# Graph network on one Trainium2 core: edge counts shared with ScalarE, ranking by predicated copies in five parts, chunk tables beside the ranking

## The reference

```python
h = jnp.maximum(_layernorm(x, axis=-1), 0.0)
# layer 0: row = src, col = dst
edge_input = jnp.concatenate([h[row], h[col], edge_attr, edge_weight / 5.0], axis=-1)
m_ij = silu(silu(edge_input @ ew1 + eb1) @ ew2 + eb2)
agg = segment_sum(m_ij, row, num_segments=n)
x = x + h + silu(concatenate([h, agg]) @ nw1 + nb1) @ nw2 + nb2
# then two attention layers over (src, dst), softmax per dst; x = x + the result
```

## Time and profile before

| | us |
|---|---|
| median of 3 runs | 8896.73 (8894.26 to 8897.62) |
| span of the profiled execution, first to last instruction | 8886.9 |
| around the span (median less span) | 9.8 |

### The profile page before, as it was taken

One profiled execution on the slowest core, in us unless ns is written; L12 is line 12 of the kernel. 1 busy time (PEld: TensorE's weight loads), 2 busy tenths in 40 slices (PEclk: granted clock), 3 DMA queues, 4 the chain that ended last, 5 costly groups with the idle time before them and its releaser, 6 DMA issues.

```text
span 8886.9 us, 230055 instructions
## 1 busy us (share of the span) xinstructions
PE 6173.7 (69%) x49885; PEld 5210.5 (59%) x50563; DVE 6168.8 (69%) x25428; ACT 4847.6 (55%) x11854; POOL 6191.5 (70%) x7562
## 2 busy tenths in 40 slices
PE   2466666666599999984666666666646666666665
PEld 2365656556588888873555555545445555656564
DVE  7799833333267676757999999999856666666665
ACT  4133333333245555534777777777647777777775
POOL 0377777777777777735777777777647777777775
PEclk9988888888899999986888888888755555555555
DMA  4233222222232323312222222222421111111114
GB/s 141 52 63 63 62 63 62 63 62 62 61 90 85 86 85 86 85 35 56 55 55 55 55 55 55 56 55 56 47 25 29 29 29 29 29 29 29 29 29 28
DMA packets 990923, 493.64 MB, mean 56 GB/s; under 512 B 830674, under 2 KB 841604, under 8 KB 990276
## 3 DMA queue, kind: packets, MB, share of 16 engines
q0 software_dynamic: 168832, 302.29, 15.6%
q1 hardware_dynamic: 701892, 169.48, 10.2%
q10 hardware_dynamic: 119840, 18.68, 1.3%
HBM read 356.53 MB, written 151.48 MB: 57 GB/s over the span
## 4 chain that ended last, share of the span: by engine, by line
issue 26%; POOL 21%; PE 20%; DVE 15%; DMA 7%; ACT 7%; DVEq 3%; ACTq 1%; POOLq 0%; SPq 0%; another core or an unknown queue 0%
POOL z_s L639 13%; POOL arena L689 8%; DMA arena<-table,arena 6%; PE ps_all L961 5%; PE ps_all L971 5%; ACT arena L825 3%; PE ps_all L984 3%; PE ps_all L981 2%; DVE arena L1494 2%; PE ps_all L1069 1%; ACT arena L857 1%; DVE arena L1580 1%; PE ps_all L993 1%; DVEq L385 1%; DVE ps_all L1232 1%
## 5 line engine op out<-in xcount | busy, mean ns | idle before, releaser
L689 POOL DMA_INDIRECT arena<-table,arena x3616 | 3527.3, 975 | 1421.4 <-issue 963.9
L639 POOL DMA_INDIRECT z_s<-arena x1660 | 1591.9, 959 | 850.8 <-issue 479.6
L1093 PE MATMUL ps_all<-arena 128*128 128x132 f32 (+1 forms) x7232 | 1584.7, 388 | 1.8 <-DVE acc L1597 1.8
L1093 PEld LDWEIGHTS ps_all<-arena 128*128 128x128 f32 x7232 | 1405.9, 288 | 2.7 <-issue 2.6
L1069 PE MATMUL ps_all<-ident_b,arena 128*128 128x128 bf16 x3616 | 465.3, 270 | 1311.8 <-DMA arena<-table,arena 1191.7
L825 ACT ACTIVATE arena<-lanes_b,arena 128x128 bf16<-128x128 bf16 x3616 | 1144.9, 386 | 349.1 <-DVE arena L1467 342.2
L1069 PEld LDWEIGHTS ps_all<-ident_b,arena 128*128 128x128 bf16 x3616 | 282.3, 117 | 1478.6 <-issue 844.4
L1494 DVE TENSOR_REDUCE arena<-ps_all 128x2 f32<-128x1024 f32 x904 | 1098.5, 1215 | 39.0 <-PE ps_all L1110 37.6
L849 ACT ACTIVATE arena<-ps_all 28x512 bf16<-28x512 bf16 (+1 forms) x904 | 527.5, 584 | 956.8 <-PE ps_all L1069 955.8
L744 ACT ACTIVATE arena<-ps_all 18x512 f32<-18x512 f32 x415 | 243.3, 586 | 1211.9 <-PE ps_all L948 1180.1
L1110 PE MATMUL ps_all<-arena,pick 128*128 128x512 bf16 x1809 | 694.6, 489 | 54.6 <-DVE arena L1494 24.3
(11 more groups left out here) (259 smaller groups left out, 15032.7 us busy)
## 6 DMA issues: line engine op xcount, KB each, us to landing
arena<-z_s SPq DMA_DIRECT2D x452, 264.0 KB, 2.7
arena<-table,arena POOLq DMA_INDIRECT x3616
arena<-rec_d SPq DMA_DIRECT2D x1660, 10.0 KB
z_s<-arena POOLq DMA_INDIRECT x1660
rec_d<-in_rec ACTq DMA_DIRECT2D x1, 16160.0 KB, 59.0
arena<-ids_d SPq DMA_DIRECT2D x904, 4.0 KB
arena<-pos_d SPq DMA_DIRECT2D x830, 0.5 KB
arena<-pos_d ACTq DMA_DIRECT2D x830, 0.5 KB
```

The lines of the kernel that those rows point to most:

```text
L639: pool.indirect_dma_start(z_s, bass.IndirectOffsetOnAxis(ap=slot[:, g.slot(SLOTS), u:u + 1], axis=0), z_out[:, g.slot(SLOTS), u, :], None) ...
L689: pool.indirect_dma_start(g_rows[:, r, u * step + CODE_WORDS:(u + 1) * step], None, tables[n], bass.IndirectOffsetOnAxis(ap=ids[:, r, 0, u ...
L1093: mm = pe.matmul(ps[6][:, 0:out_w], a_hot_f[:, g.slot(4), u, :], g_msg[:, g.slot(4), u * out_w:(u + 1) * out_w], start=(u == 0), stop=(u = ...
```

## The change

- The counts: VectorE counts 42 of the 50 source tiles; ScalarE counts the last eight with nine Sign passes over `key`, then counts `bucket`. ScalarE's own-product copies are moved in between the Sign passes, one batch after every third.
- TensorE makes all own products first, then the prefix sums, one set per count: `prefix(1)` (sources), then `prefix(0)` (destinations).
- Ranking: five parts of 186, 186, 248, 496, 496 columns. A step is compare, scan into PSUM, carry, and `copy_predicated` of the scan's result into `place` where the compare hit; the carry and the copy wait for the scan only, and the compare's tile alternates between two, so that the next compare waits for nothing.
- 24 steps of part 0 run first; then VectorE takes up the destination counts and makes tile groups, gaps, base and the three comparisons with the tile ends; then come the other 25 steps. TensorE's table matmuls run beside these.
- In the edge loop part 1 gets two steps an item for three rounds, parts 2 to 4 one step an item for six rounds each.
- `x_t` is cleared by POOL after the last Sign pass; of `z_out` only the three last columns of each row are cleared.
- The index loads are cut in five pieces instead of four.

```diff
-PARTS = (310, 434, 434, 434)
-PART_ROUNDS = 6
-RANK_STEPS = 5
+PARTS = (186, 186, 248, 496, 496)
+RANKS_A_STEP = (0, 2, 1, 1, 1)
+FIRST_RANKS = 24
+SRC_BY_ACT = 8
+RANK_STEPS = 4
...
+            pool.wait_ge(S("signs_ready"), NB + SRC_BY_ACT + 2)
+            pool.memset(x_t, 0.0).then_inc(S("x_t_clear"), 1)
             pool.wait_ge(S("blanked"), 16 * NB)
...
-            act.wait_ge(S("bucket_ready"), 1)
-            for t in range(NB + 1):
-                act.activation(hit, bucket, ACT.Sign, bias=signs_at[:, t:t + 1], accum_out=signs[:, t:t + 1]).then_inc(S("signs_ready"), 1)
-                act.wait_ge(S("signs_ready"), t + 1)
...
+            act.wait_ge(S("key_ready"), 1)
+            for t in range(SRC_BY_ACT + 1):
+                at = NB - SRC_BY_ACT + t
+                act.activation(hit, key, ACT.Sign, bias=signs_at[:, at:at + 1], accum_out=src_signs[:, t:t + 1]).then_inc(S("signs_ready"), 1)
+                act.wait_ge(S("signs_ready"), t + 1)
...
+                if t % 3 == 2 and t // 3 < len(BATCHES):
+                    own_batch(t // 3)
...
-            with link.loop(NB, 1) as b:
+            by_dve = NB - SRC_BY_ACT
+            with link.loop(by_dve, 1) as b:
...
+            def rank(k, tile, ran, turn):
...
+                found = src_hit[turn][:, 0:PARTS[k]]
+                counted = (first_counted_ps if k == 0 else counted_ps)[:, 0:PARTS[k]]
+                nought = zero if k == 0 else zero_ps
+                dve.tensor_scalar(found, keys, no, None, ALU.is_equal).then_inc(small, 1)
+                dve.wait_ge(small, ran + 1)
+                dve.tensor_tensor_scan(counted, found, nought.broadcast_to([P, PARTS[k]]), come, ALU.add, ALU.add).then_inc(small, 1)
+                dve.wait_ge(small, ran + 2)
+                dve.tensor_scalar(come, counted[:, PARTS[k] - 1:PARTS[k]], 1.0, None, ALU.mult).then_inc(small, 1)
+                dve.copy_predicated(places, found.bitcast(I32), counted).then_inc(small, 1)
...
+            with dve.Fori(0, FIRST_RANKS // 2) as b:
+                for turn in range(2):
+                    rank(0, b * 2 + turn, b * (2 * RANK_STEPS) + turn * RANK_STEPS, turn)
...
-            link(dve.memset(x_t, 0.0))
-            dve.sem_inc(S("x_t_clear"), 1)
-            link(dve.memset(z_out, 0.0))
-            assert PART_ROUNDS * SLOTS == NT - 1
-            edge_pipeline(dve, SUPER, 0, bring, cuts=[(k * PART_ROUNDS, next_part) for k in range(len(PARTS))])
+            link(dve.memset(z_out[:, :, :, F_HID + 1:], 0.0))
+            edge_pipeline(dve, SUPER, 0, bring, cuts=[(RANK_ROUND[k], next_part) for k in range(len(PARTS))])
```

More of the change, by code:

```diff
@@ L137 @@
 PART_ENDS = [(at * P // GE - SLOTS) // SLOTS for at in PART_AT]
+RANK_ROUND = [sum((NT - 1) // (SLOTS * RANKS_A_STEP[k]) for k in range(1, n)) for n in range(1, len(PARTS) + 1)]
+assert all((NT - 1) % (SLOTS * n) == 0 for n in RANKS_A_STEP[1:])
 def edges_of(a, k):
@@ L714, in own_copies, with own_batch @@
                 act.activation(own_src[:, cols, :].rearrange("p t f -> p (t f)"), ps[4][:, 0:m], ACT.Copy).then_inc(S("own_copied"), 1)
[L717 to L724 removed]
+            def own_batch(b):
+                n = len(BATCHES[b]) * P
                 act.wait_ge(S("own_t"), b + 1)
@@ L868, in _, with prefix @@
             pe.matmul(ps[6][:, 0:1], ones, falls, start=True, stop=True).then_inc(S("falls_summed"), 1)
-            pe.wait_ge(S("counts_ready"), 2)
-            for k in range(2):
+            def prefix(k):
+                pe.wait_ge(S("counts_ready"), 2 - k)
                 pe.matmul(ps[7][:, 128 * k:128 * k + NB], lower, counts[k], start=True, stop=True)
                 pe.matmul(ps[7][:, 128 * k + 64:128 * k + 64 + NB], ones, counts[k], start=True, stop=True)
-                mm = pe.matmul(ps[7][0:NB, 256 + k:257 + k], counts[k], ones[:, 0:1], start=True, stop=True)
@@ L876, in _ @@
[L876 removed]
+                pe.matmul(ps[7][0:NB, 256 + k:257 + k], counts[k], ones[:, 0:1], start=True, stop=True).then_inc(S("prefix_ready"), 1)
             pe.wait_ge(S("weights_in"), 16 * (N_WEIGHTS + 1))
             pe.wait_ge(S("h_ready"), 1)
[L879 to L895 removed]
@@ new lines, in own_transposes, with own_products @@
+            def own_transposes(b):
+                if b > 1:
+                    pe.wait_ge(S("own_tt"), b - 1)
+                for u, t in enumerate(BATCHES[b]):
+                    mm = pe.transpose(ps[b % 2][0:F_IN, u * P:(u + 1) * P], hs[:, t, :], ident)
+                mm.then_inc(S("own_t"), 1)
+            def own_products(b):
+                pe.wait_ge(S("own_tt"), b + 1)
+                if b > 0:
+                    pe.wait_ge(S("own_copied"), 2 * b)
+                for u, t in enumerate(BATCHES[b]):
+                    pe.matmul(ps[2 + b % 2][:, u * F_HID:(u + 1) * F_HID], tile_t[0:F_IN, b % 2, 0, u * P:(u + 1) * P],
+                              w_dst, start=True, stop=True)
+                    mm = pe.matmul(ps[4][:, u * F_HID:(u + 1) * F_HID], tile_t[0:F_IN, b % 2, 0, u * P:(u + 1) * P],
+                                   w_src, start=True, stop=True)
+                mm.then_inc(S("own_done"), 1)
@@ L897, in _ @@
+            own_transposes(0)
+            for b in range(len(BATCHES)):
+                if b + 1 < len(BATCHES):
+                    own_transposes(b + 1)
+                own_products(b)
+            prefix(1)
+            prefix(0)
             pe.wait_ge(S("tile_groups_ready"), 1)
@@ L1250, in _ @@
             link(dve.tensor_scalar(reached[0:NB, :], group_no[0:NB, :], tile_end[:, 0:1], None, ALU.is_ge))
+            for k in range(2):
+                link(dve.tensor_scalar(reached_groups[k], numbers, tile_end[:, k + 1:k + 2], None, ALU.is_ge))
             dve.sem_inc(S("reached_ready"), 1)
+            with dve.Fori(0, (NT - FIRST_RANKS) // 2) as b:
+                for turn in range(2):
+                    rank(0, b * 2 + (FIRST_RANKS + turn), b * (2 * RANK_STEPS) + (FIRST_RANKS + turn) * RANK_STEPS, turn)
+            rank(0, NT - 1, (NT - 1) * RANK_STEPS, 0)
+            ranked(0)
             lone = ROW_CHUNKS // 4
@@ L1334, in bring @@
                 dve.tensor_tensor(slot[:, g.slot(SLOTS)], to_spare, slot_in[:, r], ALU.add).then_inc(small, 1)
-                if 0 < ranking[0] < len(PARTS) and g.i is not None:
-                    first = SLOTS + (ranking[0] - 1) * PART_ROUNDS * SLOTS
-                    rank(ranking[0], g.at - first, g.at * RANK_STEPS + (RANK_STEPS * (NT * ranking[0] - first)))
+                k = ranking[0]
+                if 0 < k < len(PARTS) and g.i is not None:
+                    first, each = SLOTS + RANK_ROUND[k - 1] * SLOTS, RANKS_A_STEP[k]
+                    for n in range(each):
+                        tile = g.at * each + (n - first * each)
+                        rank(k, tile, g.at * (each * RANK_STEPS) + RANK_STEPS * (NT * k + n - first * each),
+                             (n if each == 2 else g.off) % 2)
             ranking = [0]
```

107 lines of the change are left out of this document (40 added, 67 removed).

## The result

The changed kernel is **slower**, by half a per cent: 8939.24 us (median of 4 runs, 8937.75 to 8943.66) against 8897.17 (4 runs, 8894.26 to 8898.97), a ratio of 1.0052 with a 95% interval of 1.004 to 1.0064. The forecast was 8816 us, faster.

The account below looks back on a forecast made before the run. POOL's scatters bound the edge loop at a fixed 2097 us, behind VectorE's preamble chain. Ranking start -21.5, steps -53.1, middle +8.5, tables -14.9 give -81 us from 8896.7: forecast 8816 us, range 8800 to 8850.

Parts of the forecast that it names:

- the time of the change is the shift of SP's first load, unless the loop slows down: Whole kernel: edge loop is a fixed 2097 us train, so the gain is the shift of SP's first record load, to 254.5.
- the clock: Rival: TensorE's stage from 2600 to 3800 us gets clock 0.84 instead of 1.00, adding 255 us: 9071 us; chance 0.02.
- A batch gives TensorE three Sign passes to be ready in, so I take no further wait: Counts in the preamble: 5.3 us a batch suffices for TensorE's own products, so VectorE goes on at 150.0 us.
- counts done: Preamble: VectorE's 42 tile counts and two small operations end at 146.0 us.
- compare to compare: Ranking in the preamble: a step takes 1.43 us instead of 2.56, plus 0.1 per loop turn; -53.1 us in all.
- predicated copy: Ranking step: copy takes 0.36 us at 186 columns, less 0.09 overlap; taken from the addition's row.
- the middle: Between the two halves of part 0's ranking: destination counts, prefix sums, moved block and comparisons add 8.5 us.
- tables: From ranking's end to SP's first record load: 19.0 us instead of 33.9, -14.9 us.
- the last of the blank groups: SP's 50 blank groups, 82.7 us, end at 236.1, 0.6 us after part 0 is ranked; costs nothing.
- The rival on dropped waits: Ranking: dropped waits bring nothing, a step is 0.24 us longer, 11.8 us in all: 8828 us; chance 0.08.
- VectorE's pace in part 1: Rival: VectorE sets the edge loop's pace from 1.77 us a ranking step; at 2.1 us, 8865 us; chance 0.08.
- The sum of -81: Whole kernel: -21.5 (start of ranking), -53.1 (steps), +8.5 (middle), -14.9 (tables) make -81 us.

Follow-up runs that it names:

- run 1: Changed kernel with VectorE's first attention loop placed to start at slot 0 of an instruction fetch block; 8815.1 us.
- runs 2: Kernel before with only VectorE's first attention loop placed at slot 100 of a fetch block; 9049.9 us.
- 10: Changed kernel with 44 one-column memsets on VectorE ahead of the first attention loop, no placing; 8822.0 us.
- 11: Kernel before with 82 one-column memsets on VectorE ahead of the first attention loop, no placing; 9013.8 us.
- run 5: Changed kernel with ScalarE's 16 MB copy of the records issued only after the weights have landed; 8920.5 us.
- run 12: Changed kernel with first attention loop at slot 0 and the predicated copy turned back into multiply and addition with waits; 8858.9 us.
- both causes away: Changed kernel with VectorE's first attention loop at slot 0 and the 16 MB record copy issued behind the weights; 8795.2 us.
- the kernel before at slot 0: Kernel before with only VectorE's first attention loop placed at slot 0 of a fetch block; 8875.4 us.
- slot 60: Changed kernel with VectorE's first attention loop starting 60 instructions into a fetch block; 8983.2 us.
- run 8: Changed kernel, loops unplaced, with a prefetch hint for the closing branch of VectorE's first attention loop; 8831.6 us.

## Why the prediction was wrong

- **The step that failed: "the time of the change is the shift of SP's first load, unless the loop slows down".** It took every stage behind the edge loop as fixed because its code is. The one of its rivals that lay outside the change's place was the clock; the place of the code was not among them, and no row on it was read. The row was there: the instruction queue and the idle time with "issue" as its end in VectorE's second-layer loop of the kernel before (235 packets and 192.3 us, above). That the first layer had next to none was luck of position (slot 8), and the change adds 211 instructions ahead of it (slot 91). Shown in its place: VectorE refetches the loop's instructions in every turn and stalls behind the taken branch, +114 us in the trace, 124 between the changed kernel and run 1, and shown both ways by runs 2, 10 and 11.
- **"A batch gives TensorE three Sign passes to be ready in, so I take no further wait"** held for 12 batches and failed for the first. TensorE's first own transposes need the weights, which land at about 81 us while ScalarE's large copy runs; before, own products began after 167 us, so no wait showed it. (The length of the copy, 59 us from issue to landing, and the engines' load beside it could have been read.) Cost 15 us at the totals (165.1 for 150.0), 18.8 us in run 5. The weights' late landing had been hidden behind other work, and the move took that cover away.
- **Right, by the rows:** counts done at 145.1 (146.0); compare to compare 1.42 and 1.51 (1.43, and 0.1 for a turn of two); predicated copy 0.36 at 186 columns, the value taken from the addition's row; ranking from 170.05 to 250.8, 80.8 us with the middle (81.0); tables 18.8 (19.0); the last of the blank groups 1 us from ranking's end; 1.265 us a scatter in all parts. The rival on dropped waits falls, since the step keeps its overlap (run 12 shows its price), and so does the one on VectorE's pace in part 1. The sum of -81 for what was summed stands at -80.2 with both causes away; that it meets to 1 us is in part luck, since it holds against the kernel before at slot 0 and not at its own place (8795.2 - 8892.7 = -97.5).
- On instruction fetch the Trainium skill ("Runtime: NRT & Kernel Launch", section "Instruction fetch mechanics") gives 512 instructions to an engine in two lines of 256, and says that a taken branch out of that window stalls. The trace agrees on the branch: the stall stands directly behind it. Two lines of 256 don't fit: the packets have 8192 bytes (2.07 MB in 253) and come five to a turn, the delays in the body are 128 instructions apart, and the loops of run 11 and of the changed kernel, 128 instructions apart, are both refetched. The measurement decides.

A refetching turn costs 2.1 us in one place and 3.2 in another (43.83 us a turn in the changed kernel, 44.47 at slot 60, 44.70 at slot 100). The stall behind the branch is the same in all three (2.9 us). What differs are VectorE's smaller idle times at the block boundaries in the body: all idle time that ends in "issue" is 4.0, 4.8 and 4.7 us a turn from 4200 to 6200 us. What stays open: why a body in four blocks is refetched without the hint and held with it, why the boundaries cost less in the changed kernel, and the 17 us that slot 0 gave to the kernel before.

## What to carry to other kernels

An edit ahead of a long loop moves it in the instruction stream, and a loop of some hundred instructions on the busiest engine can then get slower with not one instruction of it changed: here the stage lost 5 to 7% and the kernel 1.3 to 1.8%. So compare the instruction queue's packets and the "issue" idle times by stage before and after, and fix the loop's place or hint its branch before judging the edit itself. When work is moved to an earlier time, list the inputs that had long been there at the old time, and check when each lands.

## What the runs showed of the hardware

- Instructions come in packets of 8192 bytes, 128 instructions. Without a hint, VectorE's loop of 340 instructions had no packets from slots 0 and 44, where it ends within 384 slots from the start of its block, and five a turn from slots 60 and 100. The loop of 335 had five a turn from slot 52, from which it ends at 387.
- In such a turn 2.7 to 3.3 us pass from the closing branch to the next instruction in the first layer, and 2.7 to 4.0 in the second, against 0.3 without packets. In the first layer, where VectorE is busy 95% of the time, 2.1 to 3.2 us a turn reach the end; in the second, where it is busy 64%, nothing that can be seen.
- A prefetch hint on the closing branch removed the packets altogether, at a place where they came without it: 8831.6 us, 107.7 less (run 8).
- A predicated copy from PSUM takes 355 ns at 186 columns, 423 at 248 and 698 at 496, about 1.1 ns a column and 150 ns fixed; in a step of 186 columns it replaced 0.42 + 0.35 us and two waits, 0.58 us in all (run 12). These are its groups in run 1:

```profile
L1248 DVE COPY_PREDICATED acc<-acc,ps_all 128x496 f32<-128x496 int32 x98 | 68.4, 698 | 0.0
...
L1248 DVE COPY_PREDICATED acc<-acc,ps_all 128x186 f32<-128x186 int32 x98 | 34.8, 355 | 0.0
...
L1248 DVE COPY_PREDICATED acc<-acc,ps_all 128x248 f32<-128x248 int32 x49 | 20.7, 423 | 0.0
```
